# One SBUF layout for another: large tensors on multiples of 2048 bytes

## The reference

```
x = x + 0.5 * ffn(layernorm(x))
x = x + mixer(layernorm(x))
x = x + 0.5 * ffn(layernorm(x))

ffn(x):   h = silu(x @ w1.T * s1) * (x @ w2.T * s2)      # 128 -> 512
          h = gelu(h @ h1.T * s3)                        # 512 -> 512
          h = gelu(h @ h2.T * s4)                        # 512 -> 512
          return h @ w3.T * s5                           # 512 -> 128
mixer(x): h[t] = tanh((x @ B)[t] + h[t-1] @ A.T)         # 16 states, t = 0..511
          return (h @ C) @ W_out.T + b_out
```

## Time and profile before

| what | us |
|---|---|
| median of 3 runs | 387.42 |
| lowest, highest run | 387.11, 387.7 |
| span of the profiled execution, first to last instruction | 385.5 |
| PE busy | 379.3 |
| DVE busy | 279.3 |
| ACT busy | 267.8 |
| POOL busy | 163.7 |

### The profile page before, as it was taken

How to read it: one execution, slowest core, us unless ns; L and a number is a source line. 1 busy time by engine, 2 the same in 40 slices (tenths; PEclk the granted TensorE clock), 3 DMA queues, 4 the chain that set the end, 5 groups by cost and what they waited for, 6 DMA issues and landing times.

```text
span 385.5 us, 6587 instructions
## 1 busy us (share of the span) xinstructions
PE 379.3 (98%) x1793; PEld 300.7 (78%) x1793; DVE 279.3 (72%) x724; ACT 267.8 (69%) x625; POOL 163.7 (42%) x156
## 2 busy tenths in 40 slices
PE   8999999999999999999999999999999999999995
PEld 6877777778778787878778788878888788887774
DVE  4978988896777677576868866777767677676713
ACT  3789495768858687576784767858576775757554
POOL 3545261645526355142551633535334352533421
PEclk9999999999999999999999999999999999999999
DMA  7920000000000000000001001010100101000000
GB/s 235 431 101 1 27 2 27 2 2 28 2 28 2 0 27 0 28 2 28 27 2 55 2 19 38 0 54 2 48 7 0 54 0 54 0 30 26 2 28 31
DMA packets 6365, 14.00 MB, mean 36 GB/s; under 512 B 1088, under 2 KB 2112, under 8 KB 6080
## 3 DMA queue, kind: packets, MB, share of 16 engines
q1 hardware_dynamic: 5328, 13.37, 9.1%
q10 hardware_dynamic: 1008, 0.29, 0.3%
HBM read 7.37 MB, written 2.10 MB: 25 GB/s over the span
## 4 chain that ended last, share of the span: by engine, by line
PE 98%; ACT 0%; DVE 0%; issue 0%
PE F L274 75%; PE FR L274 8%; PE FR L302 2%; PE F L528 2%; PE SC L491 2%; PE SC L422 1%; PE F L519 1%; PE SC L274 1%; PE MI L302 1%; PE MI L282 1%; PE FR L292 1%; PE F L521 1%; PE SC L437 1%; PE MI L444 0%; PE MI L274 0%; PE F L546 0%
## 5 line engine op out<-in xcount | busy, mean ns | idle before, releaser
L274 PE MATMUL F<-y_hi,w_hi 128*128 128x512 f32 (+1 forms) x484 | 198.2, 410 | 0.3 <-DVE y_lo L1045 0.2
L274 PE MATMUL F<-y_lo,w_hi 128*128 128x512 f32 (+1 forms) x484 | 190.0, 393 | 0.0
L274 PEld LDWEIGHTS F<-y_hi,w_hi 128*128 128x128 f32 x484 | 91.0, 188 | 21.5 <-issue 1.9
L1213 ACT ACTIVATE y<-F,sc 128x512 f32<-128x512 f32 x111 | 76.0, 685 | 43.0 <-PE F L274 41.7
L274 PEld LDWEIGHTS F<-y_lo,w_hi 128*128 128x128 f32 x484 | 91.3, 189 | 17.1
L837 DVE TENSOR_TENSOR y_lo<-y,y_hi 128x512 fp32r<-128x512 f32 x79 | 63.9, 808 | 40.8 <-ACT y_hi L1216 40.2
L1489 POOL TENSOR_TENSOR y_lo<-y,y_hi 128x512 fp32r<-128x512 f32 x48 | 66.6, 1390 | 59.4 <-DVE y_hi L824 48.6
L1495 POOL TENSOR_TENSOR y_lo<-y,y_hi 128x512 fp32r<-128x512 f32 x48 | 62.7, 1310 | 35.2 <-ACT y_hi L1216 35.0
L1216 ACT ACTIVATE y_hi<-F,sc 128x512 fp32r<-128x512 f32 x111 | 75.9, 684 | 0.0
L1232 ACT ACTIVATE h<-SC 128x32 fp32r<-128x32 f32 x96 | 18.8, 195 | 49.5 <-PE SC L437 47.8
L274 PE MATMUL F<-xn_hi,w_hi 128*128 128x512 f32 x118 | 49.5, 419 | 0.0
(11 more groups left out here) (170 smaller groups left out, 439.5 us busy)
## 6 DMA issues: line engine op xcount, KB each, us to landing
x_all<-in_xT SPq DMA_DIRECT2D x1, 2048.0 KB, 16.9
x_all<-x1c SPq DMA_DIRECT2D x8, 256.0 KB, 2.3
x_all<-lnin SPq DMA_DIRECT2D x8, 256.0 KB, 2.3
out<-outb SPq DMA_DIRECT2D x7, 256.0 KB, 2.0
x_all<-in_xtok SPq DMA_DIRECT2D x1, 1536.0 KB, 12.6
w_raw<-in_h1T SPq DMA_DIRECT2D x2, 512.0 KB, 7.8
w_raw<-in_h2T SPq DMA_DIRECT2D x2, 512.0 KB, 9.2
x_all<-in_xtok SPq DMA_DIRECT2D x2, 128.0 KB, 2.8
```

Source lines behind the costliest of these rows:

```text
L274: mm = nc.tensor.matmul(out, wtile(w, layer, k, m), y, start=first and i == 0, stop=last and i == len(pairs) - 1)
L1213: nc.scalar.activation(y23[:, m, :], bankt[:, :], ACT.Gelu, scale=s)
```

## The change

The calls of `sb` are put in another order, and a tensor `gap` of 136 float32 per partition, which nobody reads or writes, is added. No instruction is changed.

- First come the small tensors: counters, scales, statistics, `mask`, `ones`, `b_rep`, `h_first`, `h_ne` and the like, each of 128 bytes or less, and then `gap` of 544 bytes.
- Then come all tensors whose size is a multiple of 2048 bytes: the weights `w_raw`, `w_hi`, `w_lo`, the chunks, the norms' tensors, `th`, `u` and all y tensors. With the gap they begin at 18,432 = 9 x 2048.
- Last come `ident`, `a_raw`, `a_mix`, `ct`, `wout`, `cw_rep`, `cw_mix`, the parts and `h`, of 512 to 1536 bytes.

```diff
--- before.py
+++ after.py
@@ -74,35 +74,15 @@
         HALF = KT * HID // 2
         PIECES = [(0, HID), (HID, HID)] + [(WOFF[2] + i * HALF, HALF) for i in range(4)] + [(WOFF[4], KT * P)]
         COUNTED = 5
-        w_raw = sb("w_raw", [P, WOFF[5]])
-        w_hi = sb("w_hi", [P, WOFF[5]], F32R)
-        w_lo = sb("w_lo", [P, WOFF[5]], F32R)
         ne_cnt = sb("ne_cnt", [P, len(PIECES)])
         ne_sum = sb("ne_sum", [P, 1])
         sc = sb("sc", [P, 4 * KT + 2])
         s1h = sb("s1h", [P, KT])
         s12h = sb("s12h", [P, KT])
         s3h = sb("s3h", [P, 1])
-        ident = sb("ident", [P, P])
         mask = sb("mask", [P, 6])
         ones = sb("ones", [P, 1])
-        a_raw = sb("a_raw", [P, P])
-        a_mix = sb("a_mix", [P, P], F32R)
         b_rep = sb("b_rep", [P, 2 * STATES])
-        ct = sb("ct", [P, P])
-        wout = sb("wout", [P, P])
-        cw_rep = sb("cw_rep", [P, P])
-        cw_mix = sb("cw_mix", [P, HALVES, P], F32R)
-        part_hi = sb("part_hi", [P, 2, P], F32R)
-        part_lo = sb("part_lo", [P, 2, P])
-        part_own = sb("part_own", [P, 3, P])
-
-        x_all = sb("x_all", [P, CHUNKS * N])
-        x2_all = sb("x2_all", [P, CHUNKS * N])
-        xt_all = x2_all
-        lnin = sb("lnin", [P, N])
-        x1c = sb("x1c", [P, N])
-        outb = sb("outb", [P, N])
         st_f = sb("st_f", [P, QT, 6])
         st_m = sb("st_m", [P, QT, 6])
         mv_f = sb("mv_f", [P, QT, 2])
@@ -117,18 +97,27 @@
         spare_act = sb("spare_act", [P, 1])
         mhalf = sb("mhalf", [P, QT])
         epsc = sb("epsc", [P, QT])
+        h_first = sb("h_first", [P, SCOLS], F32R)
+        h_ne = sb("h_ne", [P, SEQH, BLOCKS - 1])
+        h_nes = sb("h_nes", [P, 1])
+        again = sb("again", [1, 1], I32)
+        general = sb("general", [1, 1], I32)
+        gap = sb("gap", [P, 136])
+        w_raw = sb("w_raw", [P, WOFF[5]])
+        w_hi = sb("w_hi", [P, WOFF[5]], F32R)
+        w_lo = sb("w_lo", [P, WOFF[5]], F32R)
+        x_all = sb("x_all", [P, CHUNKS * N])
+        x2_all = sb("x2_all", [P, CHUNKS * N])
+        xt_all = x2_all
+        lnin = sb("lnin", [P, N])
+        x1c = sb("x1c", [P, N])
+        outb = sb("outb", [P, N])
         xnt_f = sb("xnt_f", [P, N])
         xnt_m = sb("xnt_m", [P, N])
         xn_hi = sb("xn_hi", [P, N], F32R)
         xn_lo = sb("xn_lo", [P, N], F32R)
         xn2 = sb("xn2", [P, N])
         xb_all = sb("xb_all", [P, CHUNKS * HCOLS])
-        h = sb("h", [P, HCOLS], F32R)
-        h_first = sb("h_first", [P, SCOLS], F32R)
-        h_ne = sb("h_ne", [P, SEQH, BLOCKS - 1])
-        h_nes = sb("h_nes", [P, 1])
-        again = sb("again", [1, 1], I32)
-        general = sb("general", [1, 1], I32)
         th = sb("th", [P, 2, N])
         u = sb("u", [P, 2, N])
         y1 = sb("y1", [P, KT, N])
@@ -139,6 +128,17 @@
         y2_lo = sb("y2_lo", [P, KT, N], F32R)
         y3_hi = sb("y3_hi", [P, KT, N], F32R)
         y3_lo = sb("y3_lo", [P, KT, N], F32R)
+        ident = sb("ident", [P, P])
+        a_raw = sb("a_raw", [P, P])
+        a_mix = sb("a_mix", [P, P], F32R)
+        ct = sb("ct", [P, P])
+        wout = sb("wout", [P, P])
+        cw_rep = sb("cw_rep", [P, P])
+        cw_mix = sb("cw_mix", [P, HALVES, P], F32R)
+        part_hi = sb("part_hi", [P, 2, P], F32R)
+        part_lo = sb("part_lo", [P, 2, P])
+        part_own = sb("part_own", [P, 3, P])
+        h = sb("h", [P, HCOLS], F32R)
 
         F = [bank(f"F{i}") for i in range(5)]
         FR = bank("FR")
```

## The result

| what | before | after |
|---|---|---|
| median of the runs, us | 387.53 | 384.49 |
| lowest, highest run, us | 387.11, 387.7 | 384.24, 385.06 |
| ratio, with its 95% interval | | 0.9922 [0.9909, 0.9934] |
| span of the profiled execution, us | 385.5 | 383.1 |
| PE busy, us | 379.3 | 376.4 |

Both kernels were timed side by side here, so the median of before is a little off the one shown above. The change makes the kernel 3.0 us faster; 6.3 us were forecast. The profiled execution of after is the slowest of its four runs (385.06 us), which is why the two spans differ by 2.4 us only. The first lines are the page of the kernel after: busy us of each engine, and the last chain. They answer.

What follows compares the result with a forecast made beforehand. PE was taken to bound the kernel, by number of matmuls times their spacing. The terms 6.9 + 0.5 - 0.6 - 0.5 gave 6.3 us, so 387.42 would become 381.1 us, range 378.3 to 387.3.

Steps and rivals of the forecast that it cites:

- Part 1: Moving operand of the y matmuls: 1144 of them each 6.0 ns shorter, 6.9 us gained.
- Part 2: The 272 xn matmuls: 2 ns each from a phase inherited from y matmuls ahead, 0.5 us gained.
- Part 3: Gain lost where PE waits: minus 0.6 us between 20 and 80 us, minus 0.5 at the scan steps.
- Part 4: Weight loads: w_hi goes from remainder 128 to 0, both multiples of 64; effect 0.
- Part 5: Casts and subtractions on ACT, DVE and POOL: taken as 0, any change hidden beside PE work.
- Part 6: First x load and closing store: taken as 0, bounded by 0.2 us either way.
- Half of it: Rival: y matmuls gain just 3 ns each, 3.4 us, giving 384.0 in 382.8 to 386; chance 0.18.
- Nothing: Rival: the remainder is innocent, no duration changes, time stays 387.4; chance 0.14.
- Slower: Rival: PE's two reads collide at equal places of 2048-byte blocks, costing 2.5 us, 389.9; chance 0.10.

Runs made afterwards that it cites:

- y_only: Kernel before with 32 unused bytes ahead of th: th, u and all y tensors move to remainder 0, weights stay at 128; 386.19 us, ratio 0.9974.
- all_32: Changed kernel with the gap 32 bytes longer: every large tensor 32 bytes off, distances as in the change; 384.42 us, ratio 0.9936.
- PE alone: Three separate kernels where only PE works, matmul streams with operands at varied addresses, some broken by small matmuls; undisturbed spacing 226.7 ns at distance 0, 233.3 at 32.
- after_again: The changed kernel run once more, unaltered, as the measure for three kernels beside it on the same chip; 384.09 us, ratio 0.9927 to before.
- w_only: Kernel before with 352 unused bytes ahead of w_raw and 1696 behind w_lo: only the weights move, remainder 128 to 480; 384.68 us, ratio 0.9937.
- y_32: Changed kernel with 32 unused bytes ahead of th and 2016 behind y3_lo: th, u and y at remainder 32; 386.60 us, ratio 0.9989 to before.
- y_64: Changed kernel with 64 unused bytes ahead of th and 1984 behind y3_lo: th, u and y at remainder 64; 385.05 us, ratio 0.9950 to before.
- the three step kernels: Changed kernel with a_mix 32 bytes off, 128 off, or 32 off plus transposed tensors 96 off; 383.57, 384.46 and 383.40 us.
- m2_distance: Separate kernel, only PE working: weights at every 32 bytes against the moving operand, streams unbroken and broken; steady spacing 226.7 ns at distance 0, 234.2 at 96.

## Why the prediction was right or wrong

**What bounds the kernel: right.** PE, by number and spacing; the windows of after still show 40.00 of 40 us, and no other engine took its place.

**Where the operands lie: the sum of addresses was right, the reading wrong.** That the y operands start 32 bytes off a multiple of 64 was taken as the cause. y_only puts them on a multiple of 2048 and gets 1.2 us; all_32 takes everything off one and keeps the gain. The cause is the distance to the weights modulo 256, 160 for y and 0 for xn before, 0 for both after. The forecast direction came out right because the change repairs both at once.

**Part 1, the step that failed: 6.0 ns for each y matmul, 6.9 us.** Measured 3.9 ns by the intervals, about 4.0 us in all. The upper bound of 6.8 ns was right for undisturbed streams (0.2266 us in the last turn of after). The 5 ns for broken stretches, from which I went up to 6.0, rested on one pair, 1.95 and 1.91 us in the earlier trace rows. After shows both eights with the same distance, 1.92 and 1.94 us, so this pair can't be read as the operand's effect alone; all 29 eights of y between two steps have 1.955 before and 1.935 after, 2.5 ns each. PE alone agrees: 1.977 us for eight matmuls and a step at distance 160, 1.958 at distance 0, 2.4 ns each. By the table of places the gain is 1.4 ns at the second and third place behind a break, 3.5 at the fourth to eighth, and 5.7 from the ninth on; scan steps and transposes leave only 370 of some 1015 y matmuls there. Even these don't average 6.0, so 6.0 lay above what the kernel's best third gets.

**Part 2, xn, 0.5 us: wrong, 0.1 measured** (230.1 to 229.7 ns). I read the 230 ns of the earlier trace rows as a phase inherited from y matmuls. The xn matmuls had distance 0 already, so what could be gained was only that. The stretch of the earlier trace rows in the profiled execution of after (timeline of PE):

```profile
212.05 0.39 PE L274 MATMUL F<-xn_hi,w_hi 128*128 128x512 f32 x1
...
213.87 0.30 PE L302 MATMUL MI<-ident,xnt_m 128*128 128x128 f32 x1
```

These eight take 1.82 us, 227 ns each, as the reading wants it; in after_again, the same kernel, they take 1.84 (211.03 to 212.87) as before, so one stretch decides nothing. By the table of places the reading holds for the xn matmuls from the ninth place on, which fell by 2.0 ns, just the forecast figure, but these are 101 of 236. The ones nearer to a break rose: by 1.0 ns at the fourth to eighth place and by 0.4 at the second and third, and the eight eights of xn between two steps went from 1.926 to 1.942 us. The forecast had no term for such a loss. The change also moved a_mix, from 64 bytes off xn's remainder to the same one; whether that is the cause stays open, since PE alone has 1.96 us at either distance.

**Part 3, what doesn't reach the end, 1.1 us: about right in sum.** Longer waits cost 0.7 and small matmuls with the scan's waits 0.6, 1.3 together; of the latter the scan wait itself is 0.4 (2.5 to 2.9, 10 to 12 waits). The early windows show their part, 0.13 and 0.09 us less busy.

**Part 4, weights: wrong in its reason.** That remainders 128 and 0 are both multiples of 64 was to mean that nothing changes. The load's duration didn't change, 188 ns both times, as the prediction had it. But w_only, which moves nothing but weights, yields 2.3 us. Their address acts on the matmul's spacing, not on the load.

**Part 5, the other engines, 0: right,** to 8 ns in the worst group of the earlier trace rows.

**Part 6, DMAs, 0 within 0.2: nothing to be seen.** The first x load takes 3.2 us to landing after, 2.8 before; but over the kernels with x at remainder 64 it takes 2.8, 2.5 and 2.5 (before, y_only, w_only), and at 0 from 2.4 to 3.2 (after, after_again, y_32, y_64 and the three step kernels), so the scatter is larger than the effect. The 0.1 us by the Trainium skill (DMA: Bandwidth & Descriptors, How a descriptor splits into AXI transactions) would drown in it, and these runs neither show nor exclude it.

**The rivals.** "Half of it" is what came: 384.5 where it had 384.0 in 382.8 to 386. Its mechanism is right in part: near a break xn's slower stretches come from something that the layout doesn't remove, far from one it did remove it. That its number is so close is partly luck, since it gave 3.4 us with nothing lost, and the trace has 4.1 gained and 1.3 lost. Its 3 ns for each y matmul were the difference of the means in the earlier trace rows, 392 against 395, the one row that covers the whole kernel, and after has just these 392. I set against it 20 intervals at 226.5 in the earlier trace rows, a stretch at the start without a step or a transpose in it. "Nothing" is excluded: 0.9922 [0.9909, 0.9934]. The rule of 16-byte lines in the Trainium skill (Advanced Engine Details and Errata, SBUF Cachelines), by which it was argued, doesn't cover this: with all starts on whole lines the spacing went from 226.7 to 234.2 ns in m2_distance. "Slower" was upside down: an equal place of weights and moving operand in their 256-byte blocks is no collision but the best case, and by 256 every weight tile of xn, not only the m = 1 tile that I named, was at xn's own remainder, which is why all of those 20 intervals were quick. 384.5 also excludes a slower kernel.

**What would show it.** Last turn at 0.2265: yes, 0.2266. y_lo at 389 to 390: no, 392. xn_lo below 392: no, 393. PE busy 40 of 40: yes. Casts unchanged: yes. Longer waits at the scan step: yes, 2.9 for 2.5 us.

## What to carry to other kernels

Where a stream of matmuls like these (128x512, this float32 format; no other was run) sets the time, compute for each pair of weights and moving operand the difference of their addresses modulo 256, and pad so that it is 0; a pad ahead of one tensor and one behind it, 2048 bytes in all (w_only), gives most of what a new layout gives. Where small matmuls break the stream often, compare the candidates with these breaks in, since their order differs from the undisturbed one. Before multiplying a gain per instruction by their number, take it from the mean over the whole kernel, or from the kind of stretch that most of them stand in: what a long undisturbed run shows is the bound, not the value. And where two operands differ in speed, list everything that differs between them, their relation to a third one too, before naming one cause.

## What the runs showed of the hardware

- Spacing of back-to-back 128x512 matmuls of this float32 format at full granted clock (2.4 GHz): 226.7 ns at distance 0, 228.8 at 192, 232.4 at 128, 233.1 to 233.3 at 32, 64, 160 and 224, 234.2 at 96, with a period of 256 bytes; 236.7 with the moving operand 4 bytes off. In periods of 2.4 GHz 226.7 ns are 544 and 233.3 are 560, 32 and 48 more than the 512 columns.
- The Trainium skill (SBUF — State Buffer, A bandwidth-pool intuition that's wrong (but worth ruling out)) gives TensorE a second, independent read port for weight loads. The spacings above don't contradict two ports, but they show that the weights' address and the stream's are not independent in time; what the two meet at, no run here shows.
- After a 32-column matmul whose weights have the stream's own remainder, a stream at distance 0 reaches 227 ns at the sixth matmul in one eight and not within eight in the next, in turn (1.95 and 1.97 us from step to step, PE alone). With the small matmul's weights 32 bytes off it does so at the second, 1.94 us each time; in the whole kernel this comes at 11 to 15 of 29 steps, for 0 to 2 otherwise.
- Two executions of one kernel don't agree in every stretch: the same eight xn matmuls took 1.82 us in after and 1.84 in after_again, with the same addresses.
